# Sixteen unread matrix products a turn in the attention stage of a one-core transformer block

## What is computed

```python
h = layernorm(x) * (1 + ca) + sa
q, k, v = split(h @ qkv_w.T + qkv_b)          # 16 heads of 8
q, k = rope(q), rope(k)
p = softmax(where(causal, q @ k.T / sqrt(8), -1e9))
x = x + ga * ((p @ v) @ proj_w.T + proj_b)
h = layernorm(x) * (1 + cb) + sb
logits = h @ router_w.T + bias                # 160 experts, top 8 of each token
x = x + gb * (routed_experts(h) + shared_expert(h))
```

## Time and profile before

| | |
|---|---|
| median of 3 runs | 1849.23 us (1842.82 to 1849.74) |
| the profiled execution, its own time | 1851.17 us |
| its span, first to last instruction | 1849.1 us |
| mean granted clock of TensorE | 0.885 of full speed |
| busy: PE, DVE, ACT, POOL | 1538.4, 1206.7, 838.0, 1028.6 us |
| turns 0 to 14, from the L599 at 84.5 us to that at 1033.6 us | 949.1 us |

### The profile page before, as it was taken

How to read it: one execution, slowest core, us unless ns; L and a number is a source line. 1 busy time by engine, 2 the same in 40 slices (tenths; PEclk the granted TensorE clock), 3 DMA queues, 4 the chain that set the end, 5 groups by cost and what they waited for, 6 DMA issues and landing times. The chain is left out here.

```text
span 1849.1 us, 34152 instructions
## 1 busy us (share of the span) xinstructions
PE 1538.4 (83%) x10822; PEld 739.3 (40%) x10822; DVE 1206.7 (65%) x4342; ACT 838.0 (45%) x1717; POOL 1028.6 (56%) x1054
## 2 busy tenths in 40 slices
PE   5577888888888887888897867896898989999976
PEld 2122334333333333333343325664444545444532
DVE  4766877877887887888778655553444545445545
ACT  1044455445545544554545544344344545444521
POOL 2001066566566656665665650007777777777776
PEclk9988778878877988998888878999899999999988
DMA  5696456556555655655564328999688889888842
GB/s 160 206 292 184 121 149 177 155 156 184 169 154 151 182 165 149 190 163 163 164 178 112 118 59 294 335 308 337 217 277 253 269 253 287 267 282 251 261 122 83
DMA packets 264986, 369.72 MB, mean 200 GB/s; under 512 B 41207, under 2 KB 141704, under 8 KB 264680
## 3 DMA queue, kind: packets, MB, share of 16 engines
q1 hardware_dynamic: 214248, 268.91, 49.2%
q0 software_dynamic: 28672, 58.78, 10.7%
q10 hardware_dynamic: 21888, 39.86, 5.8%
HBM read 219.79 MB, written 147.60 MB: 199 GB/s over the span
## 5 line engine op out<-in xcount | busy, mean ns | idle before, releaser
L1614 POOL DMA_INDIRECT vh<-results,pos_all x448 | 458.6, 1024 | 264.0 <-PE bank L1281 127.6
L571 DVE CUSTOM_DVE_ANT_0 shelf<-bank,cb_all 128x512 bf16<-128x512 f32 (+3 forms) x1024 | 443.5, 484 | 166.7 <-PE bank L561 166.0
L786 POOL DMA_INDIRECT pages<-h,pos_s x448 | 436.2, 974 | 200.6 <-issue 105.0
L675 ACT ACTIVATE prob<-bank 128x512 f32<-128x512 f32 x640 | 347.9, 598 | 316.1 <-PE bank L660 310.6
L561 PE MATMUL bank<-km,qm 64*128 64x512 bf16 (+3 forms) x1024 | 211.9, 346 | 125.5 <-DVE rmax L571 106.1
L711 PE MATMUL bank<-prob,v_ext 128*32 128x512 f32 (+3 forms) x2048 | 238.3, 548 | 6.1 <-DVE onorm L737 4.3
L1701 DVE TENSOR_TENSOR work<-work,bank 128x512 f32<-128x512 f32 x160 | 109.6, 685 | 137.8 <-ACT work L1695 131.7
L561 PEld LDWEIGHTS bank<-km,qm 64*128 64x128 bf16 x1024 | 53.8, 97 | 314.5 <-issue 153.9
L1576 ACT ACTIVATE v_ext<-bank 128x256 f32<-128x256 f32 x254 | 86.6, 382 | 201.2 <-PE bank L1562 188.1
L1624 DVE TENSOR_TENSOR vh<-vh,wts_all 128x1024 f32<-128x1024 f32 x56 | 68.7, 1226 | 157.6 <-DMA vh<-results,pos_all 157.6
L648 PE MATMUL bank<-qe,ke 64*128 64x512 bf16 (+3 forms) x1024 | 154.9, 329 | 17.6 <-DMA ke<-k_stacks 8.5
(11 more groups left out here) (211 smaller groups left out, 2422.0 us busy)
## 6 DMA issues: line engine op xcount, KB each, us to landing
prob<-wexp SPq DMA_DIRECT2D x448, 96.0 KB
pages<-free_rows SPq DMA_DIRECT2D x38, 1024.0 KB
prob<-pages SPq DMA_DIRECT2D x152, 256.0 KB, 5.1
results<-v_ext ACTq DMA_DIRECT2D x152, 256.0 KB
qm<-q_stacks SPq DMA_DIRECT2D x64, 256.0 KB, 3.9
km<-k_stacks SPq DMA_DIRECT2D x64, 256.0 KB, 5.0
qe<-q_stacks SPq DMA_DIRECT2D x64, 256.0 KB, 5.3
ke<-k_stacks SPq DMA_DIRECT2D x64, 256.0 KB, 6.0
```

The source lines that it names most:

```text
L571: last = e.tensor_tensor_reduce(out=masked[:, g % 2, c0:c0 + (i + 1) * P], in0=MX[g % 2][:, c0:c0 + (i + 1) * P], in1=mask_w[:, S - (i + 1 ...
L675: e.activation(prob[:, slot, :], ST[g % 3][:, :], ACT.Exp, scale=SCALE).then_inc(s_exa, 1)
L786: e.indirect_dma_start(out=pages, in_=h2[:, t, :], in_offset=None, out_offset=bass.IndirectOffsetOnAxis(ap=pos_s[:, t * TOPK + k:t * TOPK ...
L1614: e.indirect_dma_start(out=y8[:, i, k, :], out_offset=None, in_=results[0:ready(n) * GRP * P, :], in_offset=bass.IndirectOffsetOnAxis(ap=p ...
```

## The change

Behind the pairs of exp units with the numbers 12, 13, 17 and 18 of a turn, and behind the `attend` step that follows such a pair, one step is added for PE alone. It calls the `begin` of the next exp unit, and then makes four products of the identity with the first 512 columns of `cb_all` (128x128 by 128x512, bf16) into the bank which that exp unit overwrites. No one reads them, and they count up no semaphore. The condition `ge and gm` holds in turns 0 to 14: 60 added steps with 240 products.

```diff
+        WARM_AFTER, WARM = (12, 13, 17, 18), 4
+
+        def warm(n, g):
+
+            def pe(e):
+                begin = exp_unit(n, g)[0]
+                begin(e)
+                for _ in range(WARM):
+                    e.matmul(ST[g % 3][:, :], identb, cb_all[:, 0:S], start=True, stop=True, skip_group_check=True)
+            return pe
...
                     steps.append({"pe": pair(*units), "act": lambda e, us=units: [u[3](e) for u in us]})
                 steps += behind[1:2]
+                if ge and gm and ge[-1][1] // 2 + 5 * ((ge[0][0] + 1) % 4) in WARM_AFTER:
+                    q, u = todo_e[0]
+                    steps.append({"pe": warm(q // 4, q % 4 * UNITS + u)})
```

## The result

The changed kernel takes 1914.09 us, the median of 4 runs (1910.98 to 1921.74), against 1846.03 us for the kernel before in the same series (4 runs). The ratio is 1.037, with a 95% interval from 1.032 to 1.042: slower by 3.7%, where I had forecast 1.4% faster (1824 us against the 1849.23 us on record then). The profiled execution took 1910.98 us, with a span of 1909.1 us and a mean granted clock of 0.894, which is higher than before (0.885).

What follows compares the result with a forecast made beforehand. PE and DVE bound the kernel by turns, with a long low-clock stretch; eight turns gain 24 us, three lose 1.5, turns 0, 1 and 14 gain 3: 25.5 us off 1851.2 profiled, median 1824 us, range 1775 to 1868.

Steps and rivals of the forecast that it cites:

- What bounds the kernel: Steady turns: PE and DVE hold each other up by turns, neither the bound alone; the clock goes with turn length.
- The cost of the products: Groups behind pairs 12, 13, 17, 18: mostly hidden in PE's waits, 0.5 us a turn; 3.8 us without cover.
- Rival 4: Chance 0.19: products lie on PE's path because moved steps make ACT and PE late; all exposed 57 us, 1906 us.
- Its last number: Rival 4 with the clock's gain against full exposure of the products, 57 - 25: 1874 us or so.
- What they may bring: Clock stays high behind the second group, 2.6 us there; steady turns 61.9 us, 3.0 us less for each of eight.
- the head: Start of a steady turn: holds the rest of the 3.5 us, as its low stretches move when the turn's length does.
- The cost of the moved steps: Other streams' steps, placed a step later or so against the core by `merge`: taken as 0 on PE, ACT and SP.
- routing's transposes: On PE they go behind the next max pair; both wait for DVE there, so 0.
- ACT's halves: First split's halves (L472, L483) come together, ACT stands still for POOL: 0 to 1.6 us a turn, taken as 0.
- All three signs of being wrong: Low stretch one quad later; DVE's waits for L561 grow behind the groups; L483 waits for POOL with exponentials late behind.
- rival 3: Chance 0.16: the clock's falls only move, one stretch later at the next waits for `rmax`; 1849 to 1857 us.

Runs made afterwards that it cites:

- products_only: The same 240 products hung onto the PE part of existing steps, no step added, in the order of the kernel before: 1830.49 us, ratio 0.988 to the kernel before.
- tiny_12_13: Products in the old order behind pairs 12 and 13 only, each with 8 columns instead of 512: 1850.04 us, ratio 1.002 to the kernel before.
- products_12_13: Products in the old order, hung onto existing steps, only behind pairs 12 and 13 (120 of them): 1822.61 us, ratio 0.985 to the kernel before.
- order_only: The changed kernel with its four added steps a turn kept but no products in them: 1927.4 us, ratio 1.043 to the kernel before.
- move_pre: Kernel before, no products, only the projections' steps placed against the core as in the changed kernel: 1865.5 us, ratio 1.013.
- first_but_proj: Kernel before, no products, first half of the routing moved as in the changed kernel, but output projection and residual in their old place: ratio 1.004, on another chip.
- move_first: Kernel before, no products, only the routing's first half (output projection, second layer norm, logits) placed as in the changed kernel: 1883.61 us, ratio 1.023.
- move_second: Kernel before, no products, only the routing's second half (page counts and positions) placed as in the changed kernel: 1886.62 us, ratio 1.024.
- second_but_paging: Kernel before, no products, the routing's second half moved, but five small DVE steps of the page counts in their old place: ratio 1.005, on another chip.

## Why the prediction was wrong

**What bounds the kernel** was read rightly: PE and DVE by turns, DVE ahead of 511.0 us at a clock of 1.00 and PE behind it, with ten microseconds of work at 0.50. Eight products of L711 with 512 columns take 1.94 us in that stretch (at 513.90 us), and the same eight 1.06 us at 1.00 in products_only (L722 at 561.59). products_only has the low stretch gone from just that place, and tiny_12_13 has it back (0.51).

**The cost of the products** was 0.5 us a turn by my sum. products_12_13 and products_only lie near the gain that I had worked out (1824 us; they measure 1822.61 and 1830.49), so little of a cost shows; the four groups together take 8 us more than the two by the medians, with overlapping intervals, about the size that I gave to all of them. Rival 4 in its form of products on the path does not hold. Of the groups at half clock, to which it gave 1.9 us each, the profiled execution of the changed kernel has one, at 544.26 us, of which three products are recorded, with 1.49 us; the others take at most 1.03 us. Its last number is wrong too: 1849 with 57 - 25 us more is 1881, not 1874.

**What they may bring**: 61.9 us a turn were forecast, and a turn of products_only takes 61.4. The end of the turn gained 25.73 - 21.31 = 4.4 us where I had 2.6, and the head, for which I had 0.9, gained nothing: it took 553.43 - 513.3 = 40.1 us, with a group of products in it, against 503.87 - 464.6 = 39.3. In this turn the sum came out right by luck, by two errors that cancel.

**The cost of the moved steps** is the step that failed: the prediction says of the routing's transposes "both wait for DVE there, so I take 0", of ACT's halves "I take 0, nearer to the idle share", and has no term for DVE's own order at all. The runs put 4.3% there (order_only), some 80 us, a mean of 5.4 us for each of 15 turns. I had looked at each engine's share of idle time and taken it as slack. It was none: a step that comes late holds up what is queued behind it, and another engine then waits for that. This chain is read from the waits of the moved streams, and tested by taking steps back for two of them: the page counts, which carry 1.4 points in the changed kernel, and the output projection. Of the two terms that I did name, ACT's stand-still came to 47.2 us in 24 splits of move_pre and 15.2 us in nine turns of the changed kernel, and the transposes of the routing are not the loss of their stream: first_but_proj keeps them moved and has 1.004. Rival 4 named late ACT and PE as a way for the products to get onto the path; it had the right direction, and a wrong mechanism, since the loss needs no products. The range ended at 1868 because of the same zero: by its own bound of 1.6 us a turn it had at most 24 us for the order. All three signs of being wrong that the prediction names did appear: the low stretch stands later, DVE's waits for L561 grew by 17 us, and L483 waits for POOL, 15.2 us in ten waits.

**The clock's low stretch** in the changed kernel moved as rival 3 had it, to a later place. That PE's waits for DVE, which the moved order put there, are the reason is argued from the timeline and not shown. The products' own gain in the moved order (1.037 with them, 1.043 without) can't be told from nothing in time, as the intervals overlap, though the mean clock is higher with them: 0.889 to 0.895 in four executions, against 0.866 to 0.873.

In tiny_12_13 the low stretch (0.51 from 572.5 us) stands behind waits of PE of 0.44, 0.41, 0.80 and 0.23 us. In products_only, at the same place, the first two are gone, the wait of 0.80 us for `xn` and that of 0.23 us for `rmax` are there, and the clock is 1.00 from 556.0 to 566.0 us. So 512-column products where PE had waited 0.41 to 0.53 us kept the clock up in this turn. Whether the fall comes from such short waits or from too little work between them, no run separates.

**Open**: the loss of the projections' stream (1.3%) is told by its waits alone, and no step of it was taken back. Of the first half of the routing it is shown that the output projection carries it, not through which of its steps. And of the moved order's whole loss it is open how much is waiting and how much is the clock.

## What to carry to other kernels

A step that is added to a stream whose places are shares of its length moves everything else in the schedule; try the empty step first, and hang new work onto a step that exists. Where engines wait for each other in turn, an idle share (here 14% of PE's turn, 20% of DVE's and 50% of ACT's) is not slack for a change of order: look at which instruction is queued behind the one that comes later. Work that nobody reads paid for itself here where it filled short waits ahead of a stretch bound by TensorE, and its amount has to be tried: two products a group gave nothing that the median shows, four 1.5%, eight 0.5%.

## What was not expected of the hardware

Turns keep to a few lengths. In the traces of the kernel before, of tiny_12_13, move_pre, move_first and move_second most steady turns take 64.4 to 65.3 us, with a mean clock of 0.82 in the first two, 0.84 in move_pre and 0.87 in the last two. Most of products_only take 61.2 to 61.9 us. So waits and clock trade places within a turn, and an edit shows in how many turns have which length. Why it is so, no run here tells.

The gain does not grow with the number of products: 0.0%, 1.5% and 0.5% for two, four and eight in each of two groups, at the same place, though the four were measured on another chip.

And the same program took 2066 us on one chip (17 runs from 2061.09 to 2071.59 us) and 1847 us on the first (13 runs). Its mean granted clock was lower there, 0.848 to 0.860 against 0.886 to 0.901; the exponentials take the same 598 ns in the traces of second_but_paging on that chip and of the kernel before. The cause was not looked for.
